# Moving projection jobs between slots, weight pieces behind the opening, and routed attention ahead of two expert blocks

## The chip, the cores and the metric

The kernel runs on one core of one Trainium2 chip. The metric is the device time of the program in microseconds. The core has TensorE (PE; PEld is its weight load), VectorE (DVE), ScalarE (ACT), GpSimd (POOL) and SyncE (SP, which here only issues DMAs). Each engine works through its own list of instructions in order and waits on semaphores.

## What is computed

For each of 64 batches of 256 tokens with 256 channels the reference runs a cross-attention over 77 context rows and then a mixture of 16 experts with a causal attention in it:

```python
x = x + xattn(layernorm(x), ctx, Wq, Wk, Wv, Wo, bo)      # 8 heads of 64
h = layernorm(x)
rw = gating(h, sim_matrix, gates)                         # softmax over active experts, at least 2
q, k, v = [einsum('bte,bted->btd', rw, einsum('btc,ecd->bted', h, proj)) for proj in (q_proj, k_proj, v_proj)]
attn = softmax(causal(q @ k.T / 8)) @ v
x = x + einsum('bted,edc->btc', attn[:, :, None, :] * rw[..., None], o_proj)
```

## The kernel before

All products are made in split single precision: a value is a high and a low part, and a product takes three matmuls (`product`, lines 478 to 480). The high part is written by ACT, the low part by DVE, which subtracts it from the source.

**Stages.** Every engine's list is the function `step(i)`, called for i from -2 to 65 in the same order of stages on each engine. In step i the batch `ahead` = i+1 is in its cross-attention (`a_s` scores, `a_exp`, `a_p` on POOL, `a_pT` transposes, `a_y` the attention product with u, which ends in `x2_tiles`), `now` = i is in its routing and expert projections (`b_xT`, `b_qkv` 0 to 15, of which two, one for each half of the tokens, belong to each pair of experts; `b_top`, `b_index`, `b_route_1`, `b_route_2`, `b_w`, `b_wsum`, `b_rw` make the weights `rw`; `b_first` on ACT opens the accumulators `acc` with the first pair, and DVE adds the others), and `before` = i-1 is in the later half of its projections and in its routed attention (`c_qk` transposes q and k, `c_s` the causal scores, `c_exp`, `c_p`, `c_pT`, `c_pv`, `c_mix` multiplies by `rw_all`), `earlier` = i-2 in the output product `c_y`. The blocks "b_qkv 2" and "b_qkv 3" are the third and fourth expert block of the title. TensorE's banks are rings: `ring_b` makes b_qkv 3 (line 478, bank_b) wait for `acc_opened` of the first block, which is ACT's line 936.

**Jobs.** Context rows are projected for groups of three batches, one group in three steps: `ct` transposes the context, k0 to k3 and v0 to v3 project it, g0 to g7 (`j_g`, lines 578 and 579) multiply k by Wq, u0 to u7 (`j_u`, lines 590 and 591) multiply v by Wo. g_f needs k of f // 2, u_f needs v of f // 2. `JOBS` says in which slot of step i % 3 = 0, 1, 2 each is made; the slots E0, E1, E2, E3, M1, M2, M3, L1, L2 are places in each engine's `step`, called by `turn`. The result of a g or u job goes to the slot f % 2 of `draft` (ACT line 892 or 899, DVE line 1196 or 1203), is stored by SP to `g_dram` or `u_dram` (`store_g` line 369, `store_u` line 378), and the slot may be written again by ACT only when the store has landed (`draft_out`). `load_g` (388) and `load_u` (397, 399) bring one batch's part back. `load_u` of a new group waits for u7's store. `load_x` (353) refills `xt` once `xb_ready` says that POOL has added the bias to the last x (`a_xb`).

**Weights.** 16 pieces go through three stages (`stage`, parts of `mix` and `late_tiles`): SP loads a piece, ACT and DVE split it (`split_weights`). 0 to 5 are for the cross-attention, 6 to 13 the expert projections, 14 and 15 the output. `OPENING` is the list of the first group's jobs, ahead of the steps; before the change 6 to 10 are split in it and 11 to 15 in step -1.

Of the kernel before, what the change touches and what calls it, by code (L numbers as in the profile page):

```python
# [34 lines left out]
def xattn_moe_kernel(nc, x, ctx_in, Wq, Wk, Wv, Wo, bo, sim_matrix, gates, q_proj, k_proj, v_proj, o_proj, out, rw_dram):  # L35
# [7 lines left out]
    H = INNER // D  # L43
# [22 lines left out]
    JOBS = ({"E0": ("g", 3), "E1": ("k", 3), "E2": ("g", 4), "E3": ("g", 5), "M1": ("v", 0), "M2": ("g", 6), "L1": ("g", 7),  # L66
             "L2": ("v", 1)},
            {"E0": ("u", 0), "E1": ("u", 1), "E2": ("v", 2), "E3": ("u", 2), "M1": ("u", 3), "M2": ("v", 3), "M3": ("u", 4),
             "L1": ("ct", 0), "L2": ("u", 5)},
            {"E0": ("u", 6), "E1": ("u", 7), "E2": ("k", 0), "E3": ("k", 1), "M1": ("g", 0), "M2": ("g", 1), "L1": ("k", 2),  # L70
             "L2": ("g", 2)})
# [28 lines left out]
    def on(n):  # L100
        return 0 <= n < B

    def job(i, slot):

        if slot not in JOBS[i % 3]:
            return None
        kind, f = JOBS[i % 3][slot]
        gm = i // 3 + (2 if kind == "ct" or i % 3 == 2 and kind != "u" else 1)
        return (gm, kind, f) if 1 <= gm < GROUPS else None
# [6 lines left out]
    with es:  # L116
# [219 lines left out]

        def loads_before(piece):
            return sum(len(PIECES[k][0]) for k in range(piece % SLOTS, piece + 1, SLOTS))
# [9 lines left out]
        def _(sp):  # L348
            def load_x(n):
                if n:  # L350
                    sp.wait_ge(xb_ready, at(1, n - 1, 0))
                    sp.wait_ge(ln_done[0], at(NT, n - 1, NT - 1))
                sp.dma_start(xt[:, :, :], x[n, :, :].rearrange("(t p) c -> p t c", p=P)).then_inc(x_in, 16)
# [57 lines left out]
            def load_weights(pieces):  # L411
                for k in pieces:
                    if k >= SLOTS:
                        sp.wait_ge(wt_ready, k - SLOTS + 1)
                    for view, src in PIECES[k][0]:
                        sp.dma_start(view(stage[k % SLOTS]), src).then_inc(wt_in[k % SLOTS], 16)
# [7 lines left out]
            def step(i):  # L424
                def turn(slot):
                    if job(i, slot):
                        gm, kind, f = job(i, slot)
                        if kind == "g":
                            store_g(gm, f)
                        elif kind == "u":  # L430
                            store_u(gm, f)

                if i % 3 == 2 and i // 3 + 3 < GROUPS:
# [4 lines left out]
                if i == -1:  # L438
                    load_weights((14,))
                if on(i + 2) and i + 2 > 0:  # L440
                    load_g(i + 2)
                if i == -1:
                    load_weights((15,))
# [6 lines left out]
                turn("E3")  # L450
                turn("M1")
                turn("M2")
# [6 lines left out]
            for hc, pieces in enumerate(((6,), (7, 8), (9,), (10, 11))):  # L459
                store_g(0, 2 * hc)  # L460
                store_g(0, 2 * hc + 1)
                load_weights(pieces)
            load_g(0)
            for hc, pieces in enumerate(((12,), (13,), (), ())):
                store_u(0, 2 * hc)
                store_u(0, 2 * hc + 1)
                load_weights(pieces)
# [7 lines left out]
        def _(pe):  # L475
# [257 lines left out]
            for k, (kind, f) in enumerate(OPENING):  # L733
                if k >= A_BANKS:
                    taken(0, *OPENING[k - A_BANKS])
                if kind == "ct":
                    j_ct(0)
                    query_weights()
                elif kind == "k":
                    j_k(0, f)  # L740
                elif kind == "v":
# [85 lines left out]
        def _(act):  # L827
# [6 lines left out]
            def split_weights(k):  # L834
                hi = PIECES[k][1]
                act.wait_ge(wt_in[k % SLOTS], 16 * loads_before(k))
                nc.scalar.activation(hi, stage[k % SLOTS][:, 0:hi.shape[1]], copy).then_inc(wt_hi, 1)
# [170 lines left out]
            for kind, f in OPENING:  # L1008
                if kind == "ct":
                    j_ct(0)  # L1010
                    query_weights()
                    ln1_b(0)
                elif kind == "k":
                    j_k(0, f)
                elif kind == "v":
                    j_v(0, f)
                elif kind == "g":
                    j_g(0, f)
                else:
                    j_u(0, f)  # L1020
                for k in SPLIT_AFTER.get((kind, f), ()):
                    split_weights(k)

            def step(i):
# [22 lines left out]
                if i == -1:  # L1047
                    split_weights(11)
# [4 lines left out]
                if i == -1:  # L1053
                    split_weights(12)
                do(now, ln2_b)
                turn("E1")
                turn("E2")
# [4 lines left out]
                if i == -1:  # L1062
                    split_weights(13)
# [5 lines left out]
                turn("M1")  # L1069
                do(nxt, a_xT)  # L1070
                if i == -1:
                    split_weights(14)
# [3 lines left out]
                if i == -1:  # L1076
                    split_weights(15)
# [10 lines left out]
                do(before, c_mix, 3)  # L1088
                turn("L2")

# [5 lines left out]
        def _(dve):  # L1096
# [11 lines left out]
            def split_weights(k):  # L1108
                dve.wait_ge(wt_hi, k + 1 if k < CC else k + 1 - CC)
                for lo, hi, rows, cols in PIECES[k][2]:  # L1110
                    last = V.tensor_tensor(lo, stage[k % SLOTS][rows, cols], hi.bitcast(F32), ALU.subtract)
                last.then_inc(wt_ready, 1)
# [211 lines left out]
            def step(i):  # L1324
# [23 lines left out]
                if i == -1:  # L1348
                    split_weights(11)
# [13 lines left out]
                do(now, b_norm, 2)  # L1363
                do(before, b_qkv, 11)
                if i == -1:
                    split_weights(12)
                turn("E1")
                do(earlier, c_y)
# [6 lines left out]
                if i == -1:  # L1375
                    split_weights(13)
# [5 lines left out]
                turn("M1")  # L1382
                do(nxt, a_xT)
                if i == -1:
                    split_weights(14)
# [4 lines left out]
                if i == -1:  # L1390
                    split_weights(15)
# [14 lines left out]
                do(now, b_qkv, 5)  # L1406
                turn("L2")

# [21 lines left out]
            for kind, f in OPENING:  # L1430
                if kind == "ct":
                    j_ct(0)
                    query_weights()
                elif kind == "k":
                    j_k(0, f)
                elif kind == "v":
# [13 lines left out]
        def _(pool):  # L1450
# [110 lines left out]
            def step(i):  # L1561
# [8 lines left out]
                do(ahead, a_xb)  # L1570
# [11 lines left out]
                do(now, b_rw)  # L1582

# [33 lines left out]
```

## Time and profile before

| | before |
|---|---|
| runs (us) | 2854.28, 2860.21, 2858.8 |
| median (us) | 2858.8 |
| the profiled execution (us) | 2861.3 |
| its span, first to last instruction (us) | 2859.5 |
| its mean granted TensorE clock | 0.953 |
| busy: PE, DVE, ACT, POOL | 90%, 75%, 55%, 39% |

The profiled execution took 2.5 us more than the median. The busy shares are means over the whole span; what a wait of TensorE costs is read from the timeline of a step, which lasts some 42 us. An idle time in square brackets stands with the instruction that ended it, and behind it what released it. "issue" there means that the profile shows no releaser.

### The profile page before, as it was taken

To read this page: it belongs to the slowest core of one execution; us is meant where nothing else is said; L and a number is where in the kernel's file an instruction comes from. 1 tells how busy PE (TensorE), PEld (TensorE's weight loads), DVE (VectorE), ACT (ScalarE), POOL (GpSimd) and SP (SyncE) were. 2 spreads that over 40 slices of the span, in tenths; PEclk is the share of its full clock that TensorE was granted. 3 is DMA by queue.
4 is the path that set the end of the run, shared out by engine and by line. 5 is a ranking of instruction groups with operands and counts; after the bars stand their busy time and mean duration, and the time that the engine had idled before them with its cause. 6 is when DMAs were issued, how large, how long until landed. Compare 5 with 4: busy or idle time off the path is not lost.

```text
span 2859.5 us, 54177 instructions
## 1 busy us (share of the span) xinstructions
PE 2559.7 (90%) x17308; PEld 2482.2 (87%) x17308; DVE 2158.7 (75%) x6107; ACT 1581.5 (55%) x5110; POOL 1105.5 (39%) x1739
## 2 busy tenths in 40 slices
PE   4599898999999898999899898999989899999987
PEld 3588898989889898989899898989889899989886
DVE  5477787877787787877777787877778787878774
ACT  4565565655555565555555565555555565556542
POOL 0134344434334344434334344434434434434442
PEclk6699999999999999999999999999999999999998
DMA  7555554454554554454555554454555455465531
GB/s 197 170 155 167 159 172 139 154 179 144 169 160 156 155 165 144 149 178 143 165 152 163 162 164 142 150 179 144 171 168 161 142 170 155 147 183 149 161 107 41
DMA packets 299938, 445.78 MB, mean 156 GB/s; under 512 B 36856, under 2 KB 210872, under 8 KB 291464
## 3 DMA queue, kind: packets, MB, share of 16 engines
q1 hardware_dynamic: 230024, 374.15, 41.2%
q10 hardware_dynamic: 69632, 68.17, 10.1%
q8 instruction: 140, 2.29, 0.4%
q14 instruction: 142, 1.16, 0.1%
HBM read 257.91 MB, written 184.35 MB: 155 GB/s over the span
## 4 chain that ended last, share of the span: by engine, by line
PE 62%; issue 11%; ACT 9%; POOL 7%; DVE 6%; ACTq 3%; DMA 2%; SPq 0%; POOLq 0%; DVEq 0%
PE bank_b L478 9%; PE bank_b L479 9%; PE bank_b L480 9%; PE bank_c L478 4%; PE bank_c L479 4%; PE bank_c L480 4%; PE bank_a L478 4%; PE bank_a L479 4%; PE bank_a L480 4%; ACTq L996 3%; POOL probs L1553 2%; PE bank_a L611 2%; PE bank_a L578 1%; DVE acc L1275 1%; DMA u_dram<-draft 1%
## 5 line engine op out<-in xcount | busy, mean ns | idle before, releaser
L478 PE MATMUL bank_b<-wqkv_hi,x2T_lo 128*128 128x384 f32 (+1 forms) x2048 | 732.1, 357 | 73.3 <-ACT acc L936 73.0
L1275 DVE SCALAR_TENSOR_TENSOR acc<-bank_b,rw,acc 128x192 f32<-128x192 f32 x1792 | 653.6, 410 | 93.5 <-PE bank_b L480 89.6
L479 PE MATMUL bank_b<-wqkv_lo,x2T_hi 128*128 128x384 f32 (+1 forms) x2048 | 698.0, 341 | 0.0
L480 PE MATMUL bank_b<-wqkv_hi,x2T_hi 128*128 128x384 f32 (+1 forms) x2048 | 695.0, 339 | 0.0
L1558 POOL TENSOR_TENSOR mixs_lo<-mix,mixs_hi 128x512 fp32r<-128x512 f32 x256 | 381.0, 1520 | 428.9 <-ACT mixs_hi L1005 428.9
L478 PEld LDWEIGHTS bank_b<-wqkv_hi,x2T_lo 128*128 128x128 f32 x2048 | 391.3, 191 | 85.2 <-ACT acc L936 83.4
L906 ACT ACTIVATE probs<-bank_a,s_max 128x77 f32<-128x77 f32 x1024 | 318.5, 327 | 259.3 <-DVE s_max L1208 259.0
L479 PEld LDWEIGHTS bank_b<-wqkv_lo,x2T_hi 128*128 128x128 f32 x2048 | 391.3, 191 | 0.0
L480 PEld LDWEIGHTS bank_b<-wqkv_hi,x2T_hi 128*128 128x128 f32 x2048 | 389.1, 190 | 0.0
L1553 POOL TENSOR_TENSOR probs<-probs,p_sum 128x616 f32<-128x616 f32 x128 | 156.6, 1223 | 393.7 <-DVE p_sum L1215 393.7
L1316 DVE TENSOR_TENSOR mix<-rw_all,late_tiles 128x512 f32<-128x512 f32 x256 | 281.1, 1138 | 24.5 <-ACT late_tiles L1001 24.5
L478 PE MATMUL bank_c<-wo_hi,mixs_lo 128*128 128x256 f32 x1024 | 287.6, 281 | 3.7 <-POOL mixs_lo L1558 3.7
L480 PE MATMUL bank_c<-wo_hi,mixs_hi 128*128 128x256 f32 x1024 | 286.8, 280 | 0.0
L479 PE MATMUL bank_c<-wo_lo,mixs_hi 128*128 128x256 f32 x1024 | 286.6, 280 | 0.0
L478 PE MATMUL bank_a<-uo,pT_lo 128*128 128x256 f32 (+1 forms) x640 | 203.1, 317 | 83.4 <-issue 83.3
L1005 ACT ACTIVATE mixs_hi<-mix 128x512 fp32r<-128x512 f32 x256 | 159.8, 632 | 158.8 <-DVE mix L1316 158.8
L1538 POOL TENSOR_TENSOR mix<-acc 128x192 f32<-128x192 f32 x128 | 76.3, 596 | 374.1 <-DVE acc L1275 373.0
L478 PEld LDWEIGHTS bank_a<-uo,pT_lo 128*128 128x128 f32 (+1 forms) x640 | 142.4, 223 | 87.4 <-issue 87.0
L906 ACT ACTIVATION_READ_ACCUMULATOR probs<-bank_a,s_max 128x1 f32 x1024 | 210.9, 206 | 0.0
L1181 DVE TENSOR_TENSOR both<-bank_a,only 64x231 fp32r<-64x231 f32 x352 | 138.9, 395 | 84.1 <-ACT both L865 81.7
L479 PE MATMUL bank_a<-uo,pT_hi 128*128 128x256 f32 (+1 forms) x640 | 199.4, 312 | 0.0
L480 PE MATMUL bank_a<-uo,pT_hi 128*128 128x256 f32 (+1 forms) x640 | 198.1, 309 | 0.0
(206 smaller groups left out, 6472.6 us busy)
## 6 DMA issues: line engine op xcount, KB each, us to landing
g_dram<-draft SPq DMA_DIRECT2D x176, 462.0 KB
gq<-g_dram SPq DMA_DIRECT2D x64, 1232.0 KB, 5.7
uo<-u_dram SPq DMA_DIRECT2D x64, 1024.0 KB
rw_all<-rw_dram ACTq DMA_DIRECT2D x128, 512.0 KB, 7.1
u_dram<-draft SPq DMA_DIRECT2D x176, 308.0 KB
xt<-in_x_dram SPq DMA_DIRECT2D x64, 256.0 KB, 4.2
out_dram<-mix SPq DMA_DIRECT2D x64, 256.0 KB, 6.3
u_dram<-draft SPq DMA_DIRECT2D x88, 156.0 KB
```

Source lines behind the costliest of these rows:

```text
L478: nc.tensor.matmul(dst, lhs[1], rhs[0], start=start, stop=False)
L479: nc.tensor.matmul(dst, lhs[0], rhs[1], start=False, stop=False)
L480: return nc.tensor.matmul(dst, lhs[0], rhs[0], start=False, stop=stop)
L906: last = nc.scalar.activation(probs[:, t, h * NC:(h + 1) * NC], bank_a(f"S{j}")[:, k * NC:(k + 1) * NC], ACT.Exp, bias=s_max[:, j, k:k + 1 ...
L996: nc.scalar.dma_start(rw_all[k * D:(k + 1) * D, :, :], rw_dram[:, :].rearrange("(a k) t -> k a t", k=2)[k].partition_broadcast(D)).then_in ...
L1005: nc.scalar.activation(mixs[0][:, 2 * j:2 * j + 2, :], mix[:, 2 * j:2 * j + 2, :], copy).then_inc(mix_hi, 1)
L1181: last = V.tensor_tensor(both[rows, k, e, cols], src[rows, cols], only.bitcast(F32)[rows, k, e, cols], ALU.subtract)
L1275: V.scalar_tensor_tensor(acc[:, t, k, :], src, rw[:, t, e:e + 1], acc[:, t, k, :], ALU.mult, ALU.add).then_inc(b_evac, 1)
L1316: V.tensor_tensor(mix[:, 2 * j:2 * j + 2, :], rw_all[:, 2 * j:2 * j + 2, :], aT2[:, :].unsqueeze(1).to_broadcast([P, 2, T]), ALU.mult).the ...
L1538: G.tensor_tensor(qkv[:, t, :], acc[:, t, 0, :], acc[:, t, 1, :], ALU.add).then_inc(qkv_ready, 1)
L1553: G.tensor_tensor(part, part, p_sum[:, half, 1, :, :].unsqueeze(3).to_broadcast([P, NT, HB, NC]), ALU.mult).then_inc(p_ready, 1)
L1558: G.tensor_tensor(mixs[1][:, 2 * j:2 * j + 2, :], mix[:, 2 * j:2 * j + 2, :], mixs[0].bitcast(F32)[:, 2 * j:2 * j + 2, :], ALU.subtract).t ...
```

## The change

The jobs get other slots: u7 goes from E1 of step 2 to L2 of step 1, g0 to g3 all go into step 2, and the others move with them. On SP, `load_u` of a new group goes to the head of step 2, and `load_x` is issued behind `load_u`, ahead of L1, one step earlier than before; POOL adds the bias of that x at the end of its step. On TensorE c_s goes in front of b_qkv 2, c_pT between the two halves of `a_y`, and c_pv in front of b_qkv 3. On DVE b_top goes ahead of slot M2, c_s ahead of b_index, and c_pT ahead of `b_wsum`; on ACT c_pT goes ahead of `b_first`. The pieces 6 to 15 of the weights are split in steps -1, 0 and 1, and `query_weights` comes behind k1 in the opening, on three engines. The core of the diff:

```diff
     JOBS = (
-            {"E0": ("g", 3), "E1": ("k", 3), "E2": ("g", 4), "E3": ("g", 5), "M1": ("v", 0), "M2": ("g", 6), "L1": ("g", 7),
-             "L2": ("v", 1)},
-            {"E0": ("u", 0), "E1": ("u", 1), "E2": ("v", 2), "E3": ("u", 2), "M1": ("u", 3), "M2": ("v", 3), "M3": ("u", 4),
-             "L1": ("ct", 0), "L2": ("u", 5)},
-            {"E0": ("u", 6), "E1": ("u", 7), "E2": ("k", 0), "E3": ("k", 1), "M1": ("g", 0), "M2": ("g", 1), "L1": ("k", 2),
-             "L2": ("g", 2)})
+            {"E0": ("g", 4), "E1": ("g", 5), "E2": ("v", 0), "E3": ("g", 6), "M1": ("g", 7), "M2": ("u", 0), "L1": ("v", 1),
+             "L2": ("u", 1)},
+            {"E0": ("v", 2), "E1": ("u", 2), "E2": ("u", 3), "E3": ("v", 3), "M1": ("u", 4), "M2": ("u", 5), "M3": ("ct", 0),
+             "L1": ("u", 6), "L2": ("u", 7)},
+            {"E0": ("k", 0), "E1": ("g", 0), "E2": ("k", 1), "E3": ("g", 1), "M1": ("g", 2), "M2": ("g", 3), "L1": ("k", 2),
+             "L2": ("k", 3)})
...
+        STAGE = (0, 1, 2, 0, 1, 2, 0, 1, 2, 0, 1, 2, 1, 2, 1, 1)
...
-        SPLIT_AFTER = {("k", 1): (W_V,), ("k", 2): (W_O - 1, W_O), ("k", 3): (6,), ("v", 0): (7,), ("v", 1): (8,),
-                       ("u", 0): (9,), ("u", 2): (10,)}
+        SPLIT_AFTER = {("k", 1): (W_V,), ("k", 2): (W_O - 1, W_O)}
...
@@ SP, step @@
                 if i % 3 == 2 and i // 3 + 3 < GROUPS:
                     load_ctx(i // 3 + 3)
+                if i % 3 == 2 and on(i + 1) and i + 1 > 0:
+                    load_u(i + 1)
                 turn("E0")
-                if on(i + 2) and i + 2 > 0:
-                    load_x(i + 2)
+                weights(1, 15)
                 if on(i + 2) and i + 2 > 0:
                     load_g(i + 2)
...
                 turn("E1")
-                if i % 3 == 2 and on(i + 1) and i + 1 > 0:
-                    load_u(i + 1)
...
                 turn("M2")
-                turn("M3")
                 if i % 3 != 1 and on(i + 2):
                     load_u(i + 2)
+                if on(i + 3) and i + 3 > 0:
+                    load_x(i + 3)
                 turn("L1")
...
             load_g(0)
+            load_weights(range(6, 9))
...
@@ TensorE, step @@
                 do(now, b_qkv, 1)
+                do(before, c_s)
                 do(now, b_qkv, 2)
-                do(before, c_s)
                 fill("Y", ahead, a_y, 0)
+                do(before, c_pT)
                 do(ahead, a_y, 1)
-                do(before, c_pT)
+                do(before, c_pv)
                 do(now, b_qkv, 3)
-                do(before, c_pv)
                 do(now, b_qkv, 4)
@@ ACT, step @@
                 do(now, b_exp)
+                do(before, c_pT)
                 do(now, b_first, 0)
-                do(before, c_pT)
                 do(now, b_first, 1)
@@ DVE, step @@
                 do(before, c_qk)
+                do(now, b_top)
+                do(before, c_s)
+                do(now, b_index)
+                do(before, c_p)
                 turn("M2")
-                do(now, b_top)
-                do(now, b_index)
-                do(before, c_s)
-                do(before, c_p)
                 turn("M3")
+                do(before, c_pT)
                 do(now, b_wsum)
                 do(ahead, a_y)
-                do(before, c_pT)
@@ POOL, step @@
-                do(ahead, a_xb)
                 do(now, power, 1)
...
                 do(now, b_rw)
+                do(nxt, a_xb)
```

## Rows read from the trace of the kernel before

**Rows 1.** The page: its first line, busy time of each engine with its share of the span.

```profile
span 2859.5 us, 54177 instructions
PE 2559.7 (90%) x17308; PEld 2482.2 (87%) x17308; DVE 2158.7 (75%) x6107; ACT 1581.5 (55%) x5110; POOL 1105.5 (39%) x1739
```

**Rows 2.** TensorE's waits: engine, group, releaser: us in total, times, longest.

```profile
PE bank_a L478 <- issue: 83.3, 21, 4.9
PE bank_b L478 <- ACT acc L936: 73.0, 43, 2.0
PE bank_a L611 <- POOL probs L1553: 43.8, 21, 8.8
```

**Rows 3.** Stretches with product matmuls alone: length, PE busy, PEld busy, granted clock, DMA.

```profile
220.00:226.50 6.50, 5.25 (x30) 5.08 (x30) 0.74 0.23 76
...
2399.00:2404.00 5.00, 3.70 (x30) 3.52 (x30) 1.00 0.34 111
2772.00:2779.00 7.00, 5.29 (x30) 5.11 (x30) 0.76 0.02 5
```

**Rows 4.** Timeline, step 2, SyncE then TensorE: start, duration, operation, [idle before <-releaser].

```profile
1350.97 0.40 SPq L353 DMA_DIRECT2D xt<-in_x_dram  x1
...
1358.84 0.66 SPq L378 DMA_DIRECT2D u_dram<-draft  x2
1366.21 0.38 SPq L397 DMA_DIRECT2D uo<-u_dram  x1
...
1375.08 0.55 PE L478 MATMUL bank_a<-uo,pT_lo 128*128 128x256 f32 x1 [4.55 <-issue]
```

**Rows 5.** Timeline of DVE in the same step, at `ln1_a`.

```profile
1355.94 0.75 DVE L1126 BATCH_NORM_STATS2 stats<-xt 128x6 f32<-128x256 f32 x2 [3.15 <-DMA xt<-in_x_dram]
```

**Rows 6.** Timeline of step 1, the path from the scores to the fourth expert block.

```profile
1452.31 0.43 PE L478 MATMUL bank_b<-wqkv_hi,x2T_lo 128*128 128x400 f32 x1
...
1453.47 0.28 PE L590 MATMUL bank_a<-wo,both 128*116 128x256 f32 x1
...
1454.60 0.43 DVE L1286 TENSOR_TENSOR mixs_hi<-bank_c,mixs_hi 64x256 fp32r<-64x256 f32 x1
...
1460.79 0.19 DVE L1261 TENSOR_REDUCE w_sum<-w 128x2 f32<-128x32 f32 x1 [0.26 <-POOL w L1523]
...
1461.25 0.24 POOL L1529 TENSOR_TENSOR rw<-w,w_sum 128x32 f32<-128x32 f32 x1 [0.50 <-DVE w_sum L1263]
...
1461.53 0.73 ACT L936 ACTIVATE acc<-bank_b,rw 128x192 f32<-128x192 f32 x2 [2.26 <-POOL rw L1529]
1462.15 0.49 ACT L961 ACTIVATE mixs_lo<-bank_c 128x384 fp32r<-128x384 f32 x1
...
1462.31 0.45 PE L478 MATMUL bank_b<-wqkv_hi,x2T_lo 128*128 128x384 f32 x1 [1.72 <-ACT acc L936]
...
1462.67 0.56 DVE L1281 TENSOR_TENSOR mixs_lo<-bank_c,mixs_lo 128x384 fp32r<-128x384 f32 x1 [0.89 <-ACT mixs_lo L961]
```

**Rows 7.** A stretch behind the wait of rows 6: all engines, granted clock.

```profile
1464.00:1466.00 2.00, 2.00 (x10) 2.00 (x10) 0.79 (x3) 0.39 (x1) 0.00 (x0) 0.50 0.00 0
```

**Rows 8.** Timeline of step 1: DVE's u2 in E3, ACT's u4 in M3.

```profile
1450.77 0.68 DVE L1203 TENSOR_TENSOR draft<-bank_a,draft 116x512 fp32r<-116x512 f32 x1
...
1456.41 0.60 ACT L899 ACTIVATE draft<-bank_a 116x512 fp32r<-116x512 f32 x1 [0.78 <-DMA u_dram<-draft]
```

**Rows 9.** Timeline at the end of step 2: b_qkv 3, k2, E0's g3; DVE's k2.

```profile
1381.53 0.42 PE L478 MATMUL bank_b<-wqkv_hi,x2T_lo 128*128 128x384 f32 x1
...
1384.89 0.27 PE L553 MATMUL bank_a<-cT_hi,wk_lo 128*128 128x232 f32 x1
...
1387.98 0.27 PE L578 MATMUL bank_a<-both,wq 128*128 128x232 f32 x1
...
1389.79 0.81 DVE L1181 TENSOR_TENSOR both<-bank_a,only 64x231 fp32r<-64x231 f32 x2 [0.36 <-ACT both L865]
```

**Rows 10.** Timeline of DVE in step -1, at `ln1_a`.

```profile
98.46 0.75 DVE L1126 BATCH_NORM_STATS2 stats<-xt 128x6 f32<-128x256 f32 x2 [6.54 <-DMA xt<-in_x_dram]
```

More of the change, by code:

```diff
@@ L107, in job @@
         kind, f = JOBS[i % 3][slot]
-        gm = i // 3 + (2 if kind == "ct" or i % 3 == 2 and kind != "u" else 1)
+        gm = i // 3 + (2 if kind == "ct" or i % 3 == 2 else 1)
         return (gm, kind, f) if 1 <= gm < GROUPS else None
@@ L335, in xattn_moe_kernel @@
         assert len(PIECES) == W_O2 + 1 and all(piece[1] is None or piece[1].shape[1] <= SP_COLS for piece in PIECES)
+        STAGE = (0, 1, 2, 0, 1, 2, 0, 1, 2, 0, 1, 2, 1, 2, 1, 1)
         def loads_before(piece):
-            return sum(len(PIECES[k][0]) for k in range(piece % SLOTS, piece + 1, SLOTS))
-        SPLIT_AFTER = {("k", 1): (W_V,), ("k", 2): (W_O - 1, W_O), ("k", 3): (6,), ("v", 0): (7,), ("v", 1): (8,),
-                       ("u", 0): (9,), ("u", 2): (10,)}
+            return sum(len(PIECES[k][0]) for k in range(piece + 1) if STAGE[k] == STAGE[piece])
+        SPLIT_AFTER = {("k", 1): (W_V,), ("k", 2): (W_O - 1, W_O)}
         block = es.enter_context(nc.Block())
@@ L413, in load_weights @@
                     if k >= SLOTS:
-                        sp.wait_ge(wt_ready, k - SLOTS + 1)
+                        sp.wait_ge(wt_ready, max(p for p in range(k) if STAGE[p] == STAGE[k]) + 1)
                     for view, src in PIECES[k][0]:
-                        sp.dma_start(view(stage[k % SLOTS]), src).then_inc(wt_in[k % SLOTS], 16)
+                        sp.dma_start(view(stage[STAGE[k]]), src).then_inc(wt_in[STAGE[k]], 16)
             load_weights(range(0, 1))
@@ L450, in step @@
                 turn("E3")
+                weights(-1, 10)
                 turn("M1")
+                weights(-1, 11)
+                weights(0, 14)
                 turn("M2")
-                turn("M3")
                 if i % 3 != 1 and on(i + 2):
                     load_u(i + 2)
+                if on(i + 3) and i + 3 > 0:
+                    load_x(i + 3)
                 turn("L1")
                 turn("L2")
[L459 to L462, printed above, removed]
+            for f in range(H):
+                store_g(0, f)
             load_g(0)
[L464 to L467, printed above, removed]
+            load_weights(range(6, 9))
+            for f in range(H):
+                store_u(0, f)
             load_u(0)
@@ L737, in _ @@
                     j_ct(0)
-                    query_weights()
                 elif kind == "k":
                     j_k(0, f)
+                    if f == 1:
+                        query_weights()
                 elif kind == "v":
@@ L1010, in _ @@
                     j_ct(0)
-                    query_weights()
-                    ln1_b(0)
                 elif kind == "k":
                     j_k(0, f)
+                    if f == 1:
+                        query_weights()
+                        ln1_b(0)
                 elif kind == "v":
@@ L1088, in step @@
                 do(before, c_mix, 3)
+                if i == -1:
+                    split_weights(9)
+                if i == 0:
+                    split_weights(14)
                 turn("L2")
+                if i == -1:
+                    split_weights(10)
             for i in range(-2, B + 2):
@@ L1363, in step @@
                 do(now, b_norm, 2)
+                if i == -1:
+                    split_weights(6)
+                if i == 0:
+                    split_weights(11)
                 do(before, b_qkv, 11)
-                if i == -1:
-                    split_weights(12)
                 turn("E1")
+                if i == 1:
+                    split_weights(15)
                 do(earlier, c_y)
@@ L1406, in step @@
                 do(now, b_qkv, 5)
+                if i == -1:
+                    split_weights(9)
+                if i == 0:
+                    split_weights(14)
                 turn("L2")
+                if i == -1:
+                    split_weights(10)
             dve.wait_ge(small_in, 48)
@@ L1432, in _ @@
                     j_ct(0)
-                    query_weights()
                 elif kind == "k":
                     j_k(0, f)
+                    if f == 1:
+                        query_weights()
                 elif kind == "v":
```

52 lines of the change are left out of this document (29 added, 23 removed).

## The prediction

> **What bounds the kernel now.** I read the page first. TensorE is busy 90% of the span [rows 1], no other engine above 75%, so the question is where the missing tenth of TensorE is. The list of TensorE's own waits answers it [rows 2]: 21 waits in front of the attention product (`a_y`, 83.3 us), 43 waits of a third or fourth expert block for `acc` to be opened on ACT (73.0 us), and 21 waits of the probability transposes for GpSimd (43.8 us). There are 22 groups of three batches, so 21 means once per group and 43 means in two of a group's three steps. I call the steps by i % 3. Third, the stretches around the 21 products: 30 matmuls take 3.70 us at the full clock, but 5.25 and 5.29 us where the granted clock fell to 1.2 GHz after the wait [rows 3]. The 21 products take 3.70 to 6.54 us, mean 5.73, so 2.03 us each beyond the full-clock time.
>
> Where the product's wait comes from is seen on SyncE [rows 4]: in step 2, `u7` (slot E1) is stored at 1358.84, `load_u` waits for that store to land and is issued at 1366.21, and the product starts at 1375.08 after 4.55 us of idleness. So it is a chain of u7's slot, its store and its load, 16 us long, and the moment of its start decides. In the same step `load_x` stands behind the new context's loads and a store, at 1350.97; DVE waits 3.15 us for it at `ln1_a`, and the sums for the probabilities stand behind that on DVE, so that the transposes wait for GpSimd [rows 4, 5]. Without the three waits of the start (13.3 us) the third kind is 30.5 us in 18 waits, 1.7 us each.
>
> **The change part by part, per group.**
>
> *Slots of u.* u7 moves from E1 of step 2 to L2 of step 1, some 14 us of work earlier, and `load_u` to the head of step 2. Its chain of 16 us then ends about ten us before the product. This takes away 3.97 us of waiting (83.3 / 21) and 2.03 us of slow clock: 6.0. What is late next is the gate of the expert block, which the stall now covers in that step; it is in the sum below.
>
> *load_x one step earlier* (behind `load_u` at M2, with the `xb` add moved to GpSimd's end of the step): the load has half a step. It removes 1.7. GpSimd is free there, and SyncE's wait for `xb_ready` holds only the stores of L1 and L2, which are filled later still. I add 0.3 for the wait that k1 in E3 caused in slot M2 behind it. Sum 2.0.
>
> *The order around the scores.* Take step 1 [rows 6]. TensorE starts b_qkv 0 at 1452.31 (U), DVE has split q and k at 1455.03 (T = U + 2.72), b_qkv 3 starts at 1462.31 after 1.72 us of waiting for the first accumulator. The path to it is b_top, routing on GpSimd, `b_wsum`, `b_rw`, `b_first`. Two things change. c_s goes ahead of b_qkv 2, but needs T: two blocks of 1.16 us each end at U + 2.3, so TensorE waits about 0.55 us, 0.1 in step 1 where ct stands between. That wait is new. And DVE's slot M2 no longer stands between c_qk and b_top, so routing starts about a us earlier; but `c_pT` now stands ahead of `b_wsum` on DVE and of `b_first` on ACT. From T: c_s 0.8 and transposes 0.5 (estimates from their seven short matmuls), b_qkv 2 1.1, half of the product of [rows 3] 1.85 give T + 4.2; then ACT 0.49, DVE 0.56, `b_wsum` 0.39, GpSimd 0.31, ACT 0.77 with its hand-over [rows 6], T + 6.65 for b_qkv 3. TensorE's own work (second half of the product, c_pv moved ahead) ends at T + 6.25. The gate's wait shrinks from 1.70 to about 0.4 and now shows in all three steps. Removed 3.48 (73.0 / 21); added 3 x 0.4 and 0.55 + 0.1 + 0.55: 2.4. The old waits also cost clock: after that of rows 6 the granted clock is 0.50 [rows 7]; about ten of 43 do so, at 1.3 us, 0.6 per group. I take that as gone.
>
> *A draft slot used again too soon.* g1 (E3) and g3 (M2) of step 2 share a slot of `draft`, and g6 (E3) and u0 (M2) of step 0. Their distance is short. The nearest row is u2 to u4 of step 1 today: DVE ends at 1451.45, ACT may write again at 1456.41, 4.96 us [rows 8]. With it ACT's slot M2 ends near T + 2.1 where c_exp could start at T + 1.2; c_p and the transposes come 0.3 us late. Twice 0.3: 0.6. Nothing queued behind (c_exp, b_exp) reaches the gate sooner than that. Bounds: 0 if the store lands a us sooner, 2 x 2.75 if it takes the 7.37 us that u7's takes in rows 4.
>
> *g4 behind k2.* The change puts k2 in L1 of step 2 and g4, which reads it, in E0 of step 0. Today E0 holds g3, which reads k1. TensorE computes k2 at 1384.89 and reaches E0 at 1387.98, but DVE ends k2 at 1390.60 [rows 9]: ACT's and DVE's L1 stand behind the mixing products. From b_qkv 3 (1381.53) that is 9.07 us; with c_pT and the residual add out of the way of DVE I take 8.2. TensorE gets there in 5.4 (five blocks and slots, c_pv no longer among them). New wait 2.8 us, in front of E0. For the clock I take half of the 2.03 above: 1.0. k3 in place of g2 adds 0.1. Bounds: 0 if DVE can be that much earlier, 2.8 + 2.7 with a full fall of the clock every time.
>
> *Opening.* Five splits of ACT and DVE and their loads leave it, `query_weights` comes after k1 and delays g0 by about 3.5 us, and three pieces now stand between load_g and the u stores. I take 2 us gain there. In step -1 `load_x` stands behind four context loads, and DVE waits 6.54 us for it, until 98.46 [rows 10]; it now goes ahead of them, 5 us gain. The splits in steps 0 and 1 cost 2 back: 5 in all, between -5 and 15.
>
> Sum per group: removed 6.0 + 2.0 + 3.48 + 0.6 = 12.1; added 2.4 + 0.6 + 2.8 + 1.0 + 0.1 = 6.9. Net 5.2; times 21 is 109, with the opening 114. The profiled run took 2861.3 (span 2859.5), 2.5 above the median of 2858.8. 2861.3 - 114 = 2747 on its scale, 2745 on the median's.
>
> **Rivals.** *A, g4 does not wait.* Against: k2's row has no room. For: DVE's wait for ACT in rows 9 shows slack in the chain. It gives 3.8 x 21 = 80 more: 2665. *B, the draft ring turns into the stall, and the kernel is slower.* Place: `j_g` in ACT's M2 of step 2 and `j_u` in that of step 0, with c_exp, b_exp and the gate queued behind. Each us that the store lands later than 4.65 us after DVE moves b_qkv 3 by one, twice per group, and a third as much again for the clock; the gain of 114 is gone at about 6.6 us. At u7's 7.37 the waits cost 2 x 2.75 x 21 = 115 and the clock 42: 2902. For it: g1 leaves just behind the broadcast of the routing weights on ACT's queue. Against: u2 does the same and lands in 4.96 [rows 8]. The Trainium skill (DMA: Bandwidth & Descriptors, Queues, rings and completion order) says that each DMA engine takes the queues in turn, a packet at a time; by that rule the store shares with the broadcast as long as it lasts, which would favour B; no row here separates the two. *C, the gate's path is longer than I have it,* by 1.3 us a step (c_pT is in its way on three engines): 82 + 13 for the clock, 2840. *D, u is late all the same,* because `load_u` at the head of SyncE's step still waits: 126 back less the gate it hides, about 2845. Against it ten us of room.
>
> **Chances.** Forecast 0.68, A 0.13, B 0.07, C 0.10, D 0.02. The forecast's own range is 2700 to 2800 from its bounds; with parts of A and C, 2670 to 2830. A change within 0.2% (6 us) is about what a measurement of this kernel can tell from none. Of B, some lies near zero. Faster 0.91, same 0.02, slower 0.07.
>
> **What would show it.** Right: no wait in front of `a_y`, `load_u` issued some 15 us sooner against it; DVE never waits for xt; 21 new waits of `j_g` (L578) for `both` (L1181), near 2.8 us; waits for `acc` in all three steps but below 0.8 us; waits of c_s for DVE below 0.6 us. Wrong: long waits of ACT for g_dram or u_dram in M2, waits for `acc` still near 1.7, or no wait for k2.

## The result and the profile after

The changed kernel takes 2828.6 us (median of 4 runs, 2825.6 to 2839.3) against 2859.5 of the kernel before beside it (4 runs): a ratio of 0.990, 95% interval 0.9869 to 0.9931. It is 31 us faster where 114 were forecast. Below, its page: the first line and the busy times, to be held against [rows 1].

```profile
span 2825.1 us, 54177 instructions
PE 2542.7 (90%) x17308; PEld 2463.2 (87%) x17308; DVE 2163.9 (77%) x6107; ACT 1578.0 (56%) x5110; POOL 1108.3 (39%) x1739
```

TensorE's busy time fell by 17 us with the same 17308 matmuls. That fits the clock, whose mean granted value rose from 0.953 to 0.961. The other half of the 34 us between the spans is idle time. The list of TensorE's waits of the changed kernel (group, releaser: us in total, times, longest) answers to [rows 2]:

```profile
PE bank_c L683 <- DVE mixs_hi L1302: 79.3, 44, 5.7
PE bank_a L582 <- DVE both L1197: 55.6, 21, 2.7
PE bank_c L691 <- DVE mix L1325: 36.1, 27, 2.8
...
PE bank_b L482 <- ACT acc L941: 14.0, 61, 1.1
...
PE bank_a L615 <- POOL probs L1580: 8.1, 3, 4.2
```

The 21 stalls in front of the attention product are gone, the waits for `acc` fell from 73.0 to 14.0 us, and the probability transposes wait three times, all in the start. Three new groups stand in their place: `c_s` (L683), `g4` behind k2 (L582) and the routed transposes `c_pT` (L691). The second was forecast to a tenth of a us. The first is the surprise: in step 0 its waits are the 0.5 us of the prediction, in step 2 they are 0.6 to 5.7 us, mean 3.3.

One step 2 shows where that comes from. First SyncE's issues in it, then what ACT and TensorE do (timeline: start, duration, operation, idle time before and its releaser):

```profile
1341.50 0.39 SPq L398 DMA_DIRECT2D uo<-u_dram  x1
1341.94 0.46 SPq L400 DMA_DIRECT2D uo<-u_dram  x1
1342.52 0.35 SPq L389 DMA_DIRECT2D gq<-g_dram  x1
1342.91 0.66 SPq L370 DMA_DIRECT2D g_dram<-draft  x1
...
1342.02 0.64 DVE L1212 TENSOR_TENSOR draft<-bank_a,draft 128x462 fp32r<-128x462 f32 x1
...
1354.25 0.56 ACT L897 ACTIVATE draft<-bank_a 128x462 fp32r<-128x462 f32 x1 [4.17 <-DMA g_dram<-draft]
...
1356.34 0.38 ACT L974 ACTIVATE mixs_hi<-bank_c 64x256 fp32r<-64x256 f32 x1
...
1357.71 0.56 ACT L897 ACTIVATE draft<-bank_a 128x462 fp32r<-128x462 f32 x1 [0.99 <-DMA g_dram<-draft]
...
1357.75 0.45 PE L683 MATMUL bank_c<-mixs_hi 128*128 128x128 f32 x1 [4.14 <-DVE mixs_hi L1302]
```

DVE finishes g0 (slot E1) at 1342.66. Its store is issued at once, at 1342.91, but behind `load_u` (L398, L400) and `load_g` (L389), 2.4 MB together. ACT may write g2 (slot M1) into the same half of `draft` only at 1354.25, 11.6 us after DVE. It had waited 4.17 us. `a_xT` and `c_qk` are queued behind `j_g` on ACT, `c_s` needs `c_qk`, and TensorE stands for 4.14 us. The clock follows, as the stretch behind that wait shows (length, busy times of PE, PEld, DVE, ACT and POOL, granted clock, DMA):

```profile
1358.70:1360.80 2.10, 2.10 (x9) 2.10 (x8) 1.39 (x11) 1.11 (x5) 1.52 (x8) 0.50 0.00 0
```

That is 1.2 GHz, the lower of the two levels. The DMA engines in the 22 us from 1340, in 40 slices of 0.55 us, each digit the busy share in tenths, show why the store takes so long: they are full from the issue of the loads until 1358.

```profile
DMA  1000379998899989996999999999999940000000
```

### The profile page after: what moved, and what is told of

It is laid out like the page before. It is cut to its first block, busy times and chain, and to the rows that moved or that the text cites. A ratio compares the mean times of both kernels' runs of the same rounds, so it can differ in the third digit from the quotient of the medians.

```text
span 2825.1 us, 54177 instructions
## 1 busy us (share of the span) xinstructions
PE 2542.7 (90%) x17308; PEld 2463.2 (87%) x17308; DVE 2163.9 (77%) x6107; ACT 1578.0 (56%) x5110; POOL 1108.3 (39%) x1739
## 4 chain that ended last, share of the span: by engine, by line
PE 52%; DMA 20%; DVE 13%; ACT 9%; issue 5%; SPq 1%; POOL 1%; DVEq 0%; ACTq 0%; POOLq 0%
DMA u_dram<-draft 11%; PE bank_b L482 8%; DMA g_dram<-draft 8%; PE bank_b L483 8%; PE bank_b L484 8%; PE bank_c L482 4%; PE bank_c L483 4%; PE bank_c L484 4%; PE bank_a L482 3%; PE bank_a L483 3%; DVE acc L1291 3%; PE bank_a L484 3%; DVE mix L1332 3%; DVE mixs_lo L1297 1%; ACT mixs_lo L966 1%
## 5 line engine op out<-in xcount | busy, mean ns | idle before, releaser
L1291 DVE SCALAR_TENSOR_TENSOR acc<-bank_b,rw,acc 128x192 f32<-128x192 f32 x1792 | 661.2, 411 | 208.5 <-PE bank_b L484 190.6
L1508 POOL TENSOR_TENSOR pow_out<-pow_in,expo 128x2 f32<-128x2 f32 (+1 forms) x128 | 112.7, 881 | 299.8 <-DVE pow_in L1155 290.1
L482 PEld LDWEIGHTS bank_c<-wo_hi,mixs_lo 128*128 128x128 f32 x1024 | 197.2, 193 | 4.4 <-issue 3.9
L483 PEld LDWEIGHTS bank_c<-wo_lo,mixs_hi 128*128 128x128 f32 x1024 | 196.7, 192 | 0.0
L484 PEld LDWEIGHTS bank_c<-wo_hi,mixs_hi 128*128 128x128 f32 x1024 | 196.5, 192 | 0.0
L482 PE MATMUL bank_a<-uo,pT_lo 128*128 128x256 f32 (+1 forms) x640 | 192.6, 301 | 1.8 <-DVE xT_lo L1183 1.8
```

The lines of the kernel that those rows point to most:

```text
L482: nc.tensor.matmul(dst, lhs[1], rhs[0], start=start, stop=False)
L483: nc.tensor.matmul(dst, lhs[0], rhs[1], start=False, stop=False)
L484: return nc.tensor.matmul(dst, lhs[0], rhs[0], start=False, stop=stop)
L1291: V.scalar_tensor_tensor(acc[:, t, k, :], src, rw[:, t, e:e + 1], acc[:, t, k, :], ALU.mult, ALU.add).then_inc(b_evac, 1)
L1508: G.tensor_tensor(dst, src, expo[:, 0:m], ALU.pow).then_inc(ln_pow[k], 1)
```

## The experiments

The runs were made in three rounds, in which the kernel before took 2864.1 us (e1 to e4), 2856.4 (e5 to e8) and 2853.9 (e9 to e12), beside 2859.5 in the round of the change itself. Ratios are to the kernel before of the same round; a difference between two medians of different rounds is sure only to some 10 us.

**The draft ring.** In the timelines I read for each of the 16 blocks of a group the time from DVE's end to the moment at which ACT, having waited for it, writes the same half of `draft` again; I call it the landing of the store. In the changed kernel four stores are waited for, 21 times each: g0 lands after 10.5 us (6.1 to 13.1), g1 after 6.9 (5.2 to 8.7), g6 after 3.5 (3.1 to 5.3), u3 after 10.0 (9.4 to 11.3).

*e1.* One edit on SyncE, in step 2:

```diff
+                turn("E0")
+                weights(1, 15)
+                if i % 3 == 2:
+                    turn("E1")
                 if i % 3 == 2 and on(i + 1) and i + 1 > 0:
                     load_u(i + 1)
-                turn("E0")
-                weights(1, 15)
```

> The changed kernel with one edit on SyncE: in step 2 the store of g0 (slot E1) is issued ahead of load_u and load_g instead of behind both. Theory Q (the draft ring stalls in M1 because g0's store stands behind two loads of 2.2 MB on SyncE's queue): the store leaves within 1 us of DVE's end and lands some 5 us later, ACT's wait for g_dram in front of g2 falls from about 3.3 us a group (2.1 to 4.6) to under 0.5, TensorE's wait of c_s in step 2 falls from about 3.3 us to the 0.5 of step 0, and with the half clock behind it about 75 us go: 2755. Rival S (the store is slow by itself, as 462 KB from 128 partitions to three batches): it leaves only about 1 us sooner, so the wait shrinks by that at most: 2805 or above. Rival C (the path to the gate is the next limit at once): the wait of c_s falls, but 20 to 40 us of it come back as waits for acc: 2780.

It took 2865.5 us: 1.0002 of the kernel before, interval 0.9982 to 1.0021, so 37 slower than the changed kernel by the medians, 29 by the ratios. g0's landing did fall, to at most 7.5 us, and no g2 waited. TensorE's and ACT's waits of e1 show where the time went instead, and the timeline of one step 2 (SyncE, ACT) shows how:

```profile
PE bank_c L694 <- DVE mix L1328: 132.1, 44, 6.5
...
PE bank_c L686 <- DVE mixs_hi L1305: 23.5, 44, 2.6
...
ACT draft L900 <- DMA g_dram<-draft: 147.5, 27, 8.5
```

```profile
1360.80 0.39 SPq L370 DMA_DIRECT2D g_dram<-draft  x1
1361.31 0.42 SPq L398 DMA_DIRECT2D uo<-u_dram  x1
1361.77 0.95 SPq L400 DMA_DIRECT2D uo<-u_dram  x1
1362.83 0.35 SPq L389 DMA_DIRECT2D gq<-g_dram  x1
...
1367.99 0.63 DVE L1215 TENSOR_TENSOR draft<-bank_a,draft 128x462 fp32r<-128x462 f32 x1
...
1377.26 0.56 ACT L900 ACTIVATE draft<-bank_a 128x462 fp32r<-128x462 f32 x1 [6.06 <-DMA g_dram<-draft]
```

The stall moved one store on. `c_s` now waits 0.5 us in step 2 as it does in step 0, as expected. But the loads now run when g1 (E3) is stored; g1 lands after 9.3 us instead of 6.9, and g3 in M2 waits for it with `c_exp` queued behind on ACT. So TensorE waits in front of `c_pT`, 132 us instead of 36. Of the three cases written down none foresaw this. The cause that theory Q named fits (without the loads in front, g0's landing fell by 3 us or more) and its gain is refuted: the load had been in front of one waited store and is now in front of another.

*e2.* k2 and g3 of step 2 change places:

```diff
-             {"E0": ("k", 0), ... "M1": ("g", 2), "M2": ("g", 3), "L1": ("k", 2), "L2": ("k", 3)})
+             {"E0": ("k", 0), ... "M1": ("g", 2), "M2": ("k", 2), "L1": ("g", 3), "L2": ("k", 3)})
```

> The changed kernel with k2 and g3 of step 2 changing places (k2 in M2, g3 in L1), so that g4 in E0 of step 0 reads keys that were split five slots earlier. If k2 alone makes the wait in front of g4: 21 waits of 2.68 us and the half clock behind nine of them (1.5 us each) go, 54 + 14 = 68 us: 2760. It also takes g3's wait for g1's store out of M2 (about 1 us a group, which shows as part of TensorE's wait in front of the routed transposes): up to 15 us more. Rival: k2 has four copies on ACT and two subtractions on DVE where g3 has one and one, so c_exp starts 0.9 us later, and the wait in front of the routed transposes in step 2 grows by that, 20 us back: 2780. Rival: g4 then waits for something else, no change: 2828.

2750.6 us, 0.959 of before (0.9559 to 0.9627): 78 less than the changed kernel (88 by the ratios), more than k2's 68. The 21 waits of `g4` are gone. ACT's waits for g stores in step 2 fell from 107.1 to 75.5 us, since g3 now comes a slot later than g1's store. k2's four copies on ACT cost nothing that can be seen: `c_pT` waits 34.3 us.

*e3.* Both edits.

> Both edits together, the store of g0 ahead of the two loads and k2 in M2. If the two stalls are independent (each is in another step's neighbourhood, and between them there are 8 us of work) the gains add up: 75 + 68, 2828 - 143 = 2685. If they share a limit (the path to the gate, or DVE, which is busy 77%), the sum falls short: 2720 or more.

2666.7 us, 0.930 (0.9265 to 0.9331), 162 less than the changed kernel (172 by the ratios) and 18 below the 2685 of two gains added up. The edit that lost 37 us alone is worth 84 on top of e2, because with k2 in M2 no draft is written in that slot. What TensorE still waits for:

```profile
PE bank_c L694 <- DVE mix L1328: 34.5, 23, 2.4
PE bank_c L686 <- DVE mixs_hi L1305: 22.5, 44, 2.6
PE bank_b L485 <- ACT acc L944: 14.5, 59, 1.1
```

So the path to the gate, my rival C, is no limit: 14.5 us in all, in 59 waits.

*e7 and e8.* `load_g` goes behind the store of slot E3, without (e7) and with (e8) k2 in M2:

```diff
-                if on(i + 2) and i + 2 > 0:
-                    load_g(i + 2)
                 ...
                 turn("E3")
+                if on(i + 2) and i + 2 > 0:
+                    load_g(i + 2)
```

> The kernel of e1 (g0's store ahead of the loads), and load_g behind the store of slot E3 in every step; k2 stays in L1. In e1 the stall had moved from g2 in M1 to g3 in M2: ACT waits 6.6 us a group for g1's store, which SyncE issued right behind load_u and load_g. Theory Q (a store behind 2.2 MB of loads on the same queue lands late) says that this wait falls to about 1.5 us once only load_u is in front of it, TensorE's wait in front of c_pT from 132 us to 30 or 40, and the time from 2865 to that of e3 plus what k2 costs (56 us of wait and about 20 of clock): 2745. Rival S (g1's store needs about 7 us by itself and the gap E3 to M2 is 5 us of work): the wait stays above 5 us and the time at 2850 or above; in e3 it would then be k2's place alone that helped.

2823.4 us (0.989, 0.9871 to 0.9909), 42 less than e1 by the medians, 32 by the ratios; ACT's waits for g stores 147.5 to 103.2, `c_pT` 132.1 to 89.4, g1's landing 9.3 to 7.2 us. Theory Q holds for the 2.1 us that `load_g` added and overrates it: ACT still waits 4.7 us a group for g1's store, which needs 7 us where the way from E3 to M2 is shorter by that wait. How much of the 7 is `load_u` was not tried. Both cases of the expectation were half right.

> The kernel of e3 (g0's store ahead of the loads, k2 in M2) and load_g behind the store of slot E3 in every step. Left in e3 are ACT's waits of u5 for u3's store in step 1 (2.4 us a group), which show as 34 us in front of c_pT, and those of u0 for g6's in step 0 (0.9 us). If they too come from load_g standing in the queue ahead of these stores: 34 us fall to about 10, and c_s in step 2 to 0.5: 2667 - 30 = 2637. If they are the stores' own time (two slots, 5 to 7 us of landing): no change, 2660 to 2667. Rival: gq then comes late to the next step's S0 (25 us of room against a load of 6 to 10): waits of TensorE for g_in, above 2680.

2675.6 us (0.937, 0.9348 to 0.9386), 9 above e3 by the medians, 20 by the ratios, which between two rounds is hardly clear. u3's landing stayed (10.3 us) and g6's grew from 3.4 to 4.0. So `load_g` had nothing to do with u3's landing, and nothing was gained. That it makes g6's landing later when it is issued right behind that store is likely (e7 has the same 0.3 to 0.5 us), but no run shows it alone.

*e9.* What is beside u3's store is the broadcast of the routing weights: in the changed kernel DVE ends u3 at 1432.76, and ACT issues its two transfers, of 512 KB each (my expectation gives 512 KB for both), at 1432.13 and 1432.77. e9 is e3 with them behind `b_xT`:

```diff
                 do(ahead, a_pT, 1)
-                do(before, c_rw)
                 do(ahead, a_pT, 2)
                 ...
                 do(now, b_xT, 1)
+                do(before, c_rw)
                 turn("M1")
```

> The kernel of e3 with one edit on ACT: the two broadcasts of the routing weights (c_rw, 512 KB) are issued behind b_xT instead of between the transposes of the probabilities. In e3 and in the changed kernel u3's store lands 10.0 us after DVE (9.3 to 11.3 in 21 groups) with or without load_g in front of it, and u5 waits 2.6 us for it. It is issued within a us of the broadcasts. If they share the DMA engines with it (theory D): u3 lands after 5 to 7 us, ACT's wait in front of u5 goes, TensorE's 34.6 us in front of c_pT fall below 10, and the time to about 2635. If the store is slow by itself, because a u store is four short transfers (rival S): the landing stays near 10 and the time at 2667. Rival: rw_all comes too late for the mixing products, DVE waits for it: 2690.

2684.1 us (0.941, 0.9376 to 0.9434), 17 above e3 by the medians, 30 by the ratios. u3 now lands within 7.9 us, and its 21 waits on ACT are gone; the list of ACT's waits has only the five for u stores of the opening. But the same broadcast now meets g6's store of step 0, and that lands after 6.2 us instead of 3.4. First e3, then e9, DVE's g6, the broadcasts and ACT's u0 in one step 0:

```profile
1313.92 0.58 ACTq L1004 DMA_DIRECT2D rw_all<-rw_dram  x1
1314.53 0.66 ACTq L1004 DMA_DIRECT2D rw_all<-rw_dram  x1
...
1318.63 0.63 DVE L1215 TENSOR_TENSOR draft<-bank_a,draft 128x462 fp32r<-128x462 f32 x1
...
1322.68 0.60 ACT L907 ACTIVATE draft<-bank_a 116x512 fp32r<-116x512 f32 x1 [0.82 <-DMA g_dram<-draft]
```

```profile
1323.61 0.63 DVE L1215 TENSOR_TENSOR draft<-bank_a,draft 128x462 fp32r<-128x462 f32 x1
...
1323.45 0.58 ACTq L1004 DMA_DIRECT2D rw_all<-rw_dram  x1
1324.06 0.66 ACTq L1004 DMA_DIRECT2D rw_all<-rw_dram  x1
1324.82 0.56 ACT L900 ACTIVATE draft<-bank_a 128x462 fp32r<-128x462 f32 x1 [0.99 <-issue]
...
1330.30 0.60 ACT L907 ACTIVATE draft<-bank_a 116x512 fp32r<-116x512 f32 x1 [3.00 <-DMA g_dram<-draft]
```

Theory D is shown twice, by the store that was freed (u3, at least 2.1 us sooner) and by the one that was hit (g6, 2.8 us later): a store on SyncE's queue takes 2 to 3 us longer beside the two broadcasts on ACT's. By the rule of the Trainium skill that the prediction cites (DMA: Bandwidth & Descriptors, Queues, rings and completion order), the two queues share the engines in turn, and the traces agree.

The edit has a second cost, which the expectation did not foresee. The broadcasts are issued from ACT's own list, and that takes ACT 0.58 and 0.66 us. Behind `b_xT` they stand right ahead of slot M1, whose ACT instruction now comes after 0.99 us of idleness, and `a_xT` and `c_qk` are behind it. So `c_s` waits in all three steps, 51.4 us in 64 times against 22.5 in 44 in e3; `c_pT` loses its 33 us of step 1 and gets 25.5 in step 0.

*e10.* e3 with ct in M2 and u5 in M3 of step 1, and ACT's and DVE's slot M3 behind `b_first` and `a_y`. Here the store's landing is left alone, and the wait is taken off the path:

```diff
-            {"E0": ("v", 2), ... "M1": ("u", 4), "M2": ("u", 5), "M3": ("ct", 0), ...},
+            {"E0": ("v", 2), ... "M1": ("u", 4), "M2": ("ct", 0), "M3": ("u", 5), ...},
```

> The kernel of e3 with u5 and ct of step 1 changing places (ct in M2, u5 in M3), and ACT's and DVE's slot M3 moved behind b_first and behind the residual add of the product, so that nobody on the path to the scores and the gate waits for u3's store. It tests where the wait hurts and not how long it is. Theory: the store still lands after 10 us but u5 comes 8 us later, so the wait of ACT is gone and 34.6 us in front of c_pT with it, and a few us of clock: 2630. Rival (u6 in L1 and u7 in L2 then stand closer behind u5 and their own ring or bank waits grow): 2650 to 2667.

2634.5 us (0.923, 0.9203 to 0.926), 32 below e3 by the medians, 19 by the ratios; the waits of `c_pT` fall from 34.5 to 3.9 us. So nearly all of the 34.5 us were u3's store. e12 is e11 below with e9's late broadcast on top:

> The kernel of e11 with the broadcasts of the routing weights behind b_xT as in e9. If e9 and e10 take away the same wait, it adds nothing to e11 (within 5 us); it tells whether the late broadcast costs anything by itself once u3's store no longer matters: a DVE wait for rw_all would show as 10 us or more above e11.

2685.1 us (0.941, 0.9382 to 0.9439), 58 above e11, where I had 5 or 10. DVE does not wait for `rw_all`. The two costs of e9 are back: ACT waits for g6's store (69.9 us against 29.3), and the issue of the broadcasts delays slot M1. On TensorE `c_s` goes from 21.8 us in e11 to the first row, `c_pT` from 5.1 to the second, 50 of the 58 us together:

```profile
PE bank_c L687 <- DVE mixs_hi L1304: 48.6, 64, 2.6
PE bank_c L695 <- DVE mix L1327: 28.1, 22, 2.8
```

**The order around the scores and the slots, each alone.** e5 is the changed kernel with the order undone (on TensorE, with DVE's and ACT's to match), e6 the kernel before with that order alone:

```diff
                 do(now, b_qkv, 1)
-                do(before, c_s)
                 do(now, b_qkv, 2)
+                do(before, c_s)
                 fill("Y", ahead, a_y, 0)
-                do(before, c_pT)
                 do(ahead, a_y, 1)
-                do(before, c_pv)
+                do(before, c_pT)
                 do(now, b_qkv, 3)
+                do(before, c_pv)
```

> The changed kernel with only the order around the routed scores as it was (c_s behind b_qkv 2, c_pT behind the product, c_pv behind b_qkv 3; DVE's and ACT's order with it); slots, loads and opening stay changed. It tells what the slots with their loads do alone. Theory: the two stalls that replaced u's (ACT's wait for g0's store, DVE's k2 in front of g4) belong to the slots and stay; 21 waits of 2.7 us in front of g4 are seen again. The waits for acc grow from 14 us to between 60 and 110, since c_s and routing come later, while the 79 us in front of c_s and the 36 in front of c_pT are partly covered by b_qkv 2 and the product: between 2828 and 2870, I take 2850. Rival (the order costs as much as it gives): 2828 or less.

> The kernel before with only the order around the routed scores changed; slots, loads and opening as before. The 21 stalls in front of the attention product stay (83 us), the 43 waits for acc of 73 us fall to about 15, the clock after ten of them comes back (13 us), and waits of 0.5 us of c_s in front of DVE are new in all 64 steps (30 us), with a few us in front of c_pT. If the parts add up: 2860 - 58 - 13 + 30 + 5 = 2824, about 35 less than before, which with e5 would make the whole of the change's 31. If the u stall grows by what the gate gives (its chain of slot, store and load is one of DMA and does not move with TensorE's work): no change, 2860, since time won in front of a stall that ends at a fixed point is given back there in one step of three, so two thirds: 2836.

Both runs came out beyond what I expected (2828 to 2870, and 2824 to 2860). e5 took 2913.3 us (1.019, 1.0166 to 1.0218): the slots, loads and opening alone make the kernel before 57 us slower. e6 took 2805.1 us (0.982, 0.9804 to 0.9841): the order alone gives 51. TensorE's waits, e5 first:

```profile
PE bank_b L482 <- ACT acc L941: 96.5, 61, 2.6
PE bank_c L691 <- DVE mix L1325: 51.2, 35, 3.3
PE bank_a L582 <- DVE both L1197: 48.3, 21, 2.5
PE bank_c L683 <- DVE mixs_hi L1302: 39.3, 16, 3.8
```

```profile
PE bank_a L478 <- issue: 67.4, 21, 4.4
PE bank_a L611 <- POOL probs L1553: 50.5, 21, 8.5
PE bank_c L679 <- DVE mixs_hi L1286: 36.1, 44, 2.6
PE bank_b L478 <- ACT acc L936: 13.6, 55, 1.0
PE bank_c L687 <- DVE mix L1309: 13.4, 21, 2.4
```

In e6 the gate's waits fall as in the whole change, and the stall of u falls too, from 83.3 to 67.4. A stall of u that was fixed in time should have grown; its slot E1, its store and its load move with the work after all. In e5 the ACT and DVE waits for the draft ring are those of the changed kernel (g0's landing 10.4, u3's 10.0 us), and with the old order more of them reaches TensorE. The two parts alone sum to 6 us slower, together they are 31 faster: the order is worth 85 us on top of the changed slots and 51 on the old ones. That this comes from the late draft ring is my reading of the lists above; no run shows it alone.

**The opening.** e4 is the changed kernel with `query_weights` behind the context, and the piece loads of the start behind the u stores:

```diff
             load_g(0)
-            load_weights(range(6, 9))
             for f in range(H):
                 store_u(0, f)
             load_u(0)
+            load_weights(range(6, 9))
```

> The changed kernel with its opening half restored: query_weights right behind the context again, and the loads of the first three projection pieces behind the u stores instead of ahead of them. Theory: the opening lost 2.7 us to the kernel before although the prediction gave it 5, because g0 starts 4.5 us later (28.2 against 23.6) and because the nine piece loads stand ahead of u0's store, which makes TensorE wait 9.5 us in front of a u block. Then g0 starts near 23.7 and the first attention product near 106 to 108 instead of 112.9: 5 to 7 us, 2822. Rival: the splits of pieces 6 to 8 in step -1 then wait for their loads and hold ACT and DVE: 0 or some us slower, 2828 to 2835.

The first product starts at 108.19 us instead of 112.86 (before: 110.19), as expected, but the medians don't show it: 2830.4 us, 0.989 (0.9844 to 0.9925), with runs from 2818 to 2840. Its runs lie too far apart for 4.7 us to show. And e4 makes two edits, of which the second moves a stall: the loads now stand ahead of `load_x`, and DVE waits 7.67 us for xt in step -1 instead of 2.24. e11, which is e10 with `query_weights` back and the loads left alone, was the better test:

> The kernel of e10 with query_weights right behind the context in the opening, as it was before the change. In e4 this (with the loads of three pieces moved) brought the first attention product 4.7 us forward (112.9 to 108.2), though the medians did not show it. Expected: the first product 4 us earlier than in e10, and the time 4 us below e10's, about 2626; if the pieces' loads in front of the u stores set the opening's end by themselves: no difference.

2626.9 us (0.921, interval 0.9184 to 0.9232), 7.6 below e10 in the same round, where I had 4; the first product starts at 106.6 against 112.6. So the place of `query_weights` is worth these 6 us, and the piece loads ahead of the u stores don't take them away. This version beats both kernels. Its page:

```profile
span 2627.3 us, 54177 instructions
PE 2495.7 (95%) x17308; PEld 2420.5 (92%) x17308; DVE 2151.3 (82%) x6107; ACT 1574.0 (60%) x5110; POOL 1108.1 (42%) x1739
```

## Why the prediction was wrong

Direction right, size wrong: 83 us of the 114 are missing. By its own steps:

- *Slots of u* (6.0 a group). Right. `load_u` is issued at 1341.50, and the product of that step starts at 1360.67 without a wait.
- *load_x* (2.0). Right: no wait of the transposes after 168 us.
- *The gate* (removed 3.48, added 0.4 in each step). Too pessimistic: 14.0 us in 61 waits, 0.2 each, where the text had 25 in all. 11 us better.
- *c_s against DVE* (0.55 + 0.1 + 0.55). Right in step 0 (0.49 each) and in step 1 (none). Wrong in step 2: 3.3 us, 55 us too much. **The step that failed is the draft ring.** The text priced two pairs of slots, g1 with g3 and g6 with u0, and took one landing for both, 4.96 us, from [rows 8]. It did not list g0 (E1) with g2 (M1), nor u3 (E2) with u5 (M2), although the change makes both. They are longer apart, but their stores land after 10.5 and 10.0 us. And it took the landing for a property of the store. It is one of the place: 3.5 us for g6, 6.9 for g1, 10.5 for g0 behind two loads, in one kernel.
- *The ring's cost* (0.6 a group, 13 us in all). What it set aside shows in front of `c_pT`, and there 36.1 us were measured, 23 more than forecast. 31.4 of them stand in step 1, whose pair u3 and u5 the text had not listed, and e10 shows that they are u3's; the pairs that it priced, in steps 2 and 0, show 4.7 there.
- *g4 behind k2* (2.8 and 1.0 for the clock). 2.68 each; the clock fell behind nine of 21. The 30 matmuls from g4 on take 4.06 us at the full clock and 5.60 behind a fall, 1.5 us each: 14 us and not 21. 10 us better.
- *Clock.* The starts of successive matmuls at half speed add up to 64 us lost in the steady part, 80 before. Some 26 of the 64 lie behind 14 of the new waits of `c_s` in step 2, which the sum did not have, and 14 behind `g4`.
- *Opening* (5 us gain: 2 and 5 ahead of the first product, 2 lost behind it). Wrong in sign: the first product comes 2.7 us later. The `load_x` part held: DVE's wait for xt in step -1 fell from 6.54 to 2.24 us. `query_weights`, taken at 3.5 us, cost more: e11, which only puts it back, brings the first product forward by 6.0 us. The rest was not gained, since the nine piece loads that left the g stores now stand ahead of u0's, and TensorE waits 9.5 us in front of a u block, in e11 too, against 6.0 before. In e4 they stand behind the u stores and that wait is 5.2 us, but there they are ahead of `load_x`: DVE waits 7.67 us for xt, and the transposes 9.7. With the same opening the first product starts at 110.9 us in e3 and at 112.6 in e10, so these differences are sure to some 2 us.

The sum: 55 and 26 for `c_s` in step 2, 23 for `c_pT`, 8 for the opening, less 11 and 10: 91, where 83 are missing. The 8 us between stay open.

Rival B named the mechanism, its queue behind (`c_exp`, `b_exp` and the gate) and a threshold of 6.6 us. It took it for the M2 slots of steps 2 and 0 alone. In the changed kernel g1 lands at 6.9, beyond that threshold, and g6 at 3.5, far inside. The stall that B meant was real, but it came mostly by places that B did not name: ACT waits 3.3 us a group in M1 of step 2 (g0's store) and 2.5 in M2 of step 1 (u3's), against 1.6 and 0.9 in the M2 slots of steps 2 and 0. In e1, where g1 landed at 9.3 us, B's own place was enough: all of the gain was gone. Against B the text set [rows 8], where a store lands in 4.96 us. There ACT issues the first broadcast 5.8 us ahead of the store (kernel before, ACT and SyncE):

```profile
1445.66 0.61 ACTq L996 DMA_DIRECT2D rw_all<-rw_dram  x1
...
1451.48 2.21 SPq L378 DMA_DIRECT2D u_dram<-draft  x4
```

In the changed kernel g6 stands like that (5.4 us behind, 3.5 us to land), but u3 leaves 0.7 us behind it. The row was read without what stood beside it. Rivals A and D did not happen, and C's path had room.

## What to carry to other kernels

A ring of two buffers that a DMA empties has as many deadlines as it has reuses: list every pair of slots in the new order, with what is issued on the same queue ahead of the store and on any other queue beside it, and read its landing from a store that stands so. A stall that comes from such a ring moves to the next reuse when one store is brought forward (e1); it goes when the slot behind it writes no buffer (e3), or when its write is moved behind the work that others wait for (e10). To move the other transfer out of the store's way only chooses the next store that it meets, and its issue takes time of the engine whose list it stands in (e9, e12).

## What the runs showed of the hardware

The same 462 KB store of g lands 3.5 to 10.5 us after DVE has filled it, by what shares the DMA engines: 2.1 us more for 1.2 MB in front on the same queue (e1 against e7, g1), 2.8 us more for two broadcasts of 512 KB each beside it on another queue (e9 against e3, g6). g0's 10.5 us have both, 2.4 MB of loads ahead and the broadcasts beside it; without the loads it is at most 7.5 (e1). The issue of the two broadcasts takes ACT 1.24 us of its own list (e9). The clock was granted at the lower level behind nine of the 21 waits in front of g4 (20 of them 2.68 us), also behind two waits of `c_s` of 2.1 and 2.4 us, and in the kernel before behind one of 1.72 us [rows 6, 7]; one of 3.0 us in front of `c_s` passed without it. A stretch behind g4:

```profile
1374.50:1377.50 3.00, 3.00 (x13) 2.98 (x11) 2.52 (x7) 1.20 (x4) 0.41 (x1) 0.50 0.03 8
```

With the waits gone the clock came back as well: its mean is 0.961 in the changed kernel, 0.977 in e3 and 0.981 in e11. I have not shown what decides between the nine cases and the twelve.
